# Stage 1 of a four-layer network: one x tile on its own transfer, one bias product, ternary weights two steps earlier, the first turns of stage 2 in four banks

## The reference

```python
# layer 1: attention inside one row (32 heads of 16, 4 groups)
q = x @ Wq + bq; kv = x @ Wkv + bkv          # 512 and 128 columns
scores = einsum(q, k) / 4; out = softmax(scores) * v
# layer 2: feed-forward with ternary weights
quant(w) = clip(round(w / (mean(|w|) + 1e-8)), -1, 1)
h = sigmoid(x @ quant(w1).T) * (x @ quant(w2).T); f = h @ quant(w3).T   # 1408 hidden
# layer 3: causal attention with rotary positions, 16 heads of 32
# layer 4: silu(x @ w_gate) * (x @ w_up), the 2 largest of each 4 kept, @ w_down
```

## Time and profile before

| | |
|---|---|
| median of 3 runs | 1456.96 us (1456.81 to 1458.09) |
| the profiled execution's own time | 1460.82 us |
| its span, first to last instruction | 1458.8 us |
| mean granted TensorE clock | 0.977 of full |
| busy: PE, DVE, ACT, POOL | 1362.8, 1019.7, 662.4, 684.3 us |
| step 0 to the first product of `up2(0)` | 0 to 128.25 us |

### The profile page before, as it was taken

One profiled execution on the slowest core, in us unless ns is written; L12 is line 12 of the kernel. 1 busy time (PEld: TensorE's weight loads), 2 busy tenths in 40 slices (PEclk: granted clock), 3 DMA queues, 4 the chain that ended last, 5 costly groups with the idle time before them and its releaser, 6 DMA issues.

```text
span 1458.8 us, 19653 instructions
## 1 busy us (share of the span) xinstructions
PE 1362.8 (93%) x7214; PEld 926.6 (64%) x7238; DVE 1019.7 (70%) x2118; ACT 662.4 (45%) x1150; POOL 684.3 (47%) x836
## 2 busy tenths in 40 slices
PE   6997999999989899989999998989999999999997
PEld 5984445555455454554554436878888888878885
DVE  5896566665657777777857645487678867887776
ACT  5664233232323544445543574455545545454442
POOL 2575122312313223234232357567768768666862
PEclk9998999999998899999999999999999999999999
DMA  9100210112213111133120401532223222332300
GB/s 341 49 1 1 73 58 1 44 58 89 79 44 95 52 45 37 45 85 106 38 74 1 139 30 59 195 122 87 87 87 144 87 103 102 143 125 106 116 29 29
DMA packets 46248, 116.87 MB, mean 80 GB/s; under 512 B 3399, under 2 KB 4425, under 8 KB 42313
## 3 DMA queue, kind: packets, MB, share of 16 engines
q1 hardware_dynamic: 45080, 114.31, 23.2%
q10 hardware_dynamic: 1072, 1.31, 0.3%
HBM read 92.28 MB, written 23.07 MB: 79 GB/s over the span
## 4 chain that ended last, share of the span: by engine, by line
PE 64%; DVE 24%; ACT 5%; POOL 3%; issue 2%; DMA 1%; SPq 0%; POOLq 0%; DVEq 0%; ACTq 0%
PE PS L1634 63%; DVE cm L615 5%; DVE PS L817 2%; DVE SM L631 2%; DVE SM L627 2%; PE PS L1643 1%; DVE tm L615 1%; DVE SM L621 1%; ACT EX L1218 1%; POOL SM L1449 1%; DVE hm L624 1%; DVE RD L853 1%; DMA rw<-in_L_ffn_w_up 1%; DVE SM L632 1%; DVE qb L621 1%
## 5 line engine op out<-in xcount | busy, mean ns | idle before, releaser
L1218 ACT ACTIVATE EX<-PS 128x512 f32<-128x512 f32 (+3 forms) x384 | 170.2, 495 | 167.9 <-PE PS L1634 166.5
L1449 POOL TENSOR_TENSOR SM<-SM 128x1 f32<-128x1 f32 x256 | 108.6, 427 | 258.0 <-DVE SM L621 248.0
L1449 POOL TENSOR_TENSOR ws_g<-rw,ws_g 128x512 fp32r<-128x512 f32 x64 | 137.2, 2144 | 131.2 <-ACT ws_g L1045 131.2
L1634 PE MATMUL PS<-KG,QG 96*128 96x512 f32 (+3 forms) x384 | 144.8, 399 | 27.1 <-DVE SM L817 15.8
L1553 POOL TENSOR_SCALAR_AFFINE_SELECT EX<-EX 128x128 f32<-128x128 f32 x256 | 75.8, 306 | 198.3 <-ACT EX L1218 194.5
L817 DVE CUSTOM_DVE_ANT_0 PS<-PS,MW 128x128 f32<-128x128 f32 (+3 forms) x256 | 122.2, 498 | 35.0 <-PE PS L1634 34.2
L1634 PE MATMUL PS<-QG,KG 98*128 98x512 f32 (+3 forms) x384 | 136.9, 384 | 4.9 <-ACT EX L1218 2.8
L1418 ACT ACTIVATE ab<-hm 128x512 f32<-128x512 f32 x64 | 40.5, 633 | 209.0 <-DVE hm L615 209.0
L1634 PE MATMUL PS<-ws_d,HH 128*128 128x512 f32 x528 | 125.7, 389 | 0.2 <-DVE HH L615 0.2
L627 DVE TENSOR_REDUCE SM<-PS 128x1 f32<-128x512 f32 x128 | 87.3, 682 | 50.7 <-PE PS L1634 50.4
L1634 PEld LDWEIGHTS PS<-QG,KG 98*128 98x128 f32 x384 | 72.8, 194 | 77.7 <-issue 48.1
(11 more groups left out here) (201 smaller groups left out, 2819.4 us busy)
## 6 DMA issues: line engine op xcount, KB each, us to landing
rw<-in_L_ffn_w_gate SPq DMA_DIRECT2D x16, 1024.0 KB, 5.1
rw<-in_L_ffn_w_up SPq DMA_DIRECT2D x16, 1024.0 KB, 5.1
rw<-in_L_ffn_w_down SPq DMA_DIRECT2D x16, 1024.0 KB, 7.0
QG<-qs SPq DMA_DIRECT2D x48, 256.0 KB, 4.3
raw<-in_L_ffn_w SPq DMA_DIRECT2D x3, 2816.0 KB, 19.8
qs<-stg SPq DMA_DIRECT2D x16, 512.0 KB, 3.8
xA<-xs SPq DMA_DIRECT2D x2, 2048.0 KB, 9.1
ys<-xA SPq DMA_DIRECT2D x4, 1024.0 KB, 5.8
```

Of the source, the lines that this page charges most:

```text
L1218: e.activation(EX[:, n % 16, 0:W], PS[:, score_bank(n), 0:W], ACT.Exp, scale=ISQ, bias=0.0).then_inc(S["ex"], 1)
L1449: return e.tensor_tensor(out, a, b, op)
L1634: return e.matmul(out, l, r, start=start, stop=stop, skip_group_check=free)
```

## The change

1. x tile 1 has its own transfer straight behind tile 0; tiles 2 and 3 follow where 1 to 3 were. In step 1, DVE takes tile 1's statistics before `weights1`, not after.
2. raw1 is issued only when raw0 has landed. Tiles 8 to 15 stay behind it.
3. The bias rows are loaded at partitions 0 and 32 (two transfers more); the high half is in row 0 and the low half in row 32 of a tile that DVE first fills with zeros (33 x 640), and one product per bank over 33 rows takes the place of two. ACT makes two copies in place of one.
4. Sums, means, compares, turns and copies of the ternary weights are all two steps earlier (the first sums one step); statistics and norms of the first four tiles of layer 2 too. The last turns are now all ahead of `up2(0)`.
5. The first two turns of stage 2 use banks 4 and 5 and wait only for tile 14's scores; the next two use 6 and 7.
6. DVE's `softmax1(6)` and ACT's norms of tiles 10 and 11 move from step 20 to behind the first four turns.
7. In every layernorm of the kernel (128 of them), DVE no longer writes the negated mean; POOL's last instruction forms the shift from mean and scale in one `tensor_scalar` in place of a `tensor_tensor`.

```diff
@@ sp_program
             e.dma_start(xA[:, 0:1, :], xin[:, 0:1, :]).then_inc(S["d_x0"], 16)
-            e.dma_start(BR[0:1, :, 0:256], bq_d...).then_inc(S["d_b"], 16)
-            e.dma_start(BR[0:1, :, 256:320], bkv_d...).then_inc(S["d_b"], 16)
+            e.dma_start(xA[:, 1:2, :], xin[:, 1:2, :]).then_inc(S["d_x1"], 16)
+            for r in (0, 32):
+                e.dma_start(BR[r:r + 1, :, 0:256], bq_d...).then_inc(S["d_b"], 16)
+                e.dma_start(BR[r:r + 1, :, 256:320], bkv_d...).then_inc(S["d_b"], 16)
             w.wait_ge(S["d_wqa"], 32)
-            e.dma_start(xA[:, 1:4, :], xin[:, 1:4, :]).then_inc(S["d_x1"], 16)
+            e.dma_start(xA[:, 2:4, :], xin[:, 2:4, :]).then_inc(S["d_x2"], 16)
             e.dma_start(raw[0]..., w1_d...).then_inc(S["d_raw0"], 16)
             e.dma_start(xA[:, 4:8, :], xin[:, 4:8, :])
+            w.wait_ge(S["d_raw0"], 16)
             e.dma_start(raw[1]..., w2_d...).then_inc(S["d_raw1"], 16)
@@ sums: 4, 4, 5, 5 (were 5, 5, 6, 6) for m = 0; else
-    range(4 * m + 3, 4 * m + 7)
+    range(4 * m + 2, 4 * m + 6)
@@ bank3, freed
-            return 6 + misc_no[t] % 2 if t in misc_no else top_no[t] % 3
+            return (misc_no[t] + 4 if misc_no[t] < 2 else 6 + misc_no[t] % 2) if t in misc_no else top_no[t] % 3
+            if x < 2 and t in misc_no:
+                return "pr", NT - (x < 0)
@@ dve_program
-                ts1(col(n, 2), col(n, 1), float(eps), ALU.add)
-                ts1(col(n, 3), col(n, 0), -1.0, ALU.mult).then_inc(S[sem], 1)
+                ts1(col(n, 2), col(n, 1), float(eps), ALU.add).then_inc(S[sem], 1)
+            e.memset(BRH[:, :, :].bitcast(F32), 0.0)
-                        tt(BRH[:, 1], BR[:, :, :], BRH[:, 0], ALU.subtract).then_inc(S["wlo"], 1)
+                        tt(BRH[32:33], BR[32:33], bhi[32:33], ALU.subtract).then_inc(S["wlo"], 1)
             for s in range(21):
-                if 16 <= s < 20: ... stats(32 + s - 16, xt(s - 16), EPS, "mv3")
-                if s == 1: weights1()
-                if s in (7, 11, 15): gamma_sum((s - 7) // 4)
-                if s in (8, 12, 16): gamma((s - 8) // 4)
+                if 14 <= s < 18: ... stats(32 + s - 14, xt(s - 14), EPS, "mv3")
+                if s in (6, 10, 14): gamma_sum((s - 6) // 4)
+                if s in (7, 11, 15): gamma((s - 7) // 4)
                 phase1(s)
-                if 0 <= s - 9 < 12: quantize(s - 9)
+                if s == 1: weights1()
+                if 0 <= s - 7 < 12: quantize(s - 7)
@@ act_program
-                        cp(BRH[:, 0], BR[:, :, :]).then_inc(S["whi"], 1)
+                        cp(BRH[0:1], BR[0:1])
+                        cp(bhi[32:33], BR[32:33]).then_inc(S["whi"], 1)
@@ pool_program
-                tt(col(n, 5), col(n, 3), col(n, 4), ALU.mult).then_inc(S[sem], 1)
+                e.tensor_scalar(col(n, 5), col(n, 0), col(n, 4), -1.0, ALU.mult, ALU.mult).then_inc(S[sem], 1)
@@ pe_program
                 for a in range(2):
-                    for hl in range(2):
-                        mm(out[a], onesr[0:1, :], BRH[0:1, hl, a, :], hl == 0, False)
+                    mm(out[a], onesr[0:33, :], BRH[:, a, :], True, False)
             for s in range(21):
-                if s in (8, 12, 16): gamma((s - 8) // 4)
-                quantized(s - 11, 2)
+                if s < 20: quantized(s - 9, 2)
                 ... project1, transpose4 ...
-                quantized(s - 10, 0)
-                quantized(s - 10, 1)
+                quantized(s - 8, 0)
+                quantized(s - 8, 1)
+                if s in (6, 10, 14): gamma((s - 6) // 4)
@@ ahead of up2(0), and in its first turns
-            for i in range(4): turn_x(i)
+            turn_x(0); turn_x(1); quantized(11, 2); turn_x(2); turn_x(3)
-                if n == 0: quantized(10, 2); quantized(11, 0)
-                if n == 1: quantized(11, 1); quantized(11, 2)
```

More of the change, by code:

```diff
@@ L216, in network @@
         turns = []
[L217 to L220, removed]
+        for s in range(21):
+            turns += [("t", gdone[s - 9] + 2)] if 0 <= s - 9 < 12 and groups[s - 9] == 3 else []
+            turns += [("t", gdone[s - 8] + k) for k in range(2)] if 0 <= s - 8 < 12 else []
+            turns += [("s", (s - 6) // 4)] if s in (6, 10, 14) else []
         turn_no = {t: n for n, t in enumerate(turns)}
@@ L224, in turn_bank @@
             return 2 + turn_no[t] % 2
-        sums = [(s, m, k) for m in range(3) for k, s in enumerate((5, 5, 6, 6) if m == 0 else range(4 * m + 3, 4 * m + 7))]
+        sums = [(s, m, k) for m in range(3) for k, s in enumerate((4, 4, 5, 5) if m == 0 else range(4 * m + 2, 4 * m + 6))]
         jobs = {10 + c: ("q", c) for c in range(4)}
@@ L707, in phase1 @@
                     scores1(at_k[5])
-                if 7 in at_k and at_k[7] % 2:
+                if 7 in at_k and at_k[7] % 2 and step != 20:
                     softmax1(at_k[7] // 2)
@@ L1111, in phase1, with norms1 @@
                     norm(xn1[:, i % 2, :], xt(i), i).then_inc(S["xn1"], 1)
-                if 9 in at_k and at_k[9] % 2:
-                    for i in (at_k[9] - 1, at_k[9]):
-                        w.wait_ge(S["rs2"], i + 1)
-                        w.wait_ge(S["x1"], max(0, i - 1))
-                        norm(yn1[:, i % 2, :], o0[:, i % 4, :], 16 + i).then_inc(S["yn1"], 1)
+                if 9 in at_k and at_k[9] % 2 and step != 20:
+                    norms1(at_k[9])
+            def norms1(last):
+                for i in (last - 1, last):
+                    w.wait_ge(S["rs2"], i + 1)
+                    w.wait_ge(S["x1"], max(0, i - 1))
+                    norm(yn1[:, i % 2, :], o0[:, i % 4, :], 16 + i).then_inc(S["yn1"], 1)
             def norm2(i):
@@ L1356, in split_w @@
                 cp(hi, src).then_inc(S["h" + ("w" if kind == "d" else kind)], 1)
-            for i in range(4):
-                turn_x(i)
+            turn_x(0)
+            turn_x(1)
+            quantized(11, 1)
+            turn_x(2)
+            turn_x(3)
+            norms1(11)
             for n in range(44):
@@ L1933, in down4 @@
                         last.then_inc(S["dd"], 1)
-            for i in range(4):
-                turn_x(i)
+            turn_x(0)
+            turn_x(1)
+            quantized(11, 2)
+            turn_x(2)
+            turn_x(3)
             for n in range(44):
```

76 lines of the change are left out of this document (36 added, 40 removed).

## The result

| | before | after |
|---|---|---|
| median | 1456.88 us (1456.45 to 1458.09, 4 runs) | 1446.72 us (1444.73 to 1449.17, 4 runs) |
| ratio, 95% interval | | 0.9923 [0.9909, 0.9938] |
| profiled execution, its span | 1460.82, 1458.8 us | 1444.73, 1443.0 us |
| `up2(0)` starts | 128.25 us | 120.34 us |
| `up2(2)` starts | 142.45 us | 130.67 us |

The change takes 10.2 us; 10.4 were forecast, and 1446.5 us as the time. The interval of the ratio lies clear of 1, so the change is faster, by 0.8%.

The account below looks back on a forecast made before the run. Stage 1 was taken as PE-bound to 44 us, then DVE-bound to 128; 2.0 + 1.3 - 1.2 + 2.75 + 1.75 + 0.7 = 7.3 us at `up2(0)`, plus 2.8 and 0.3, gave 10.4 us: 1446.5 us, range 1441.5 to 1452.

Parts of the forecast that it names:

- moved turns: On PE, the last four groups move ahead of `up2(0)` into idle holes, bringing `up2(2)` 2.8 us more.
- Rival C: POOL's new two-scalar instruction is slow; 1.2 us more per set on the path spends the advance; chance 0.05.
- The clock: At `up2(0)`, PE's clock taken to be low again, so no term; if not, 2.95 us more.
- rival A: Clock stays at 2.4 GHz through `up2(0)`, 2.95 us more gain, 1443.5 us; chance 0.27.
- Rival B: In stage 1, DVE or ACT waits, such as for a late raw1, eat the advance: about 1451 us; chance 0.18.
- Rival D: PE and DVE are so evenly loaded that the wait only changes its name; nothing moves; chance 0.05.

Follow-up runs that it names:

- run 2: Changed kernel with tiles 1 to 3 again in one transfer behind the weights and tile 1's statistics after `weights1`: 1453.33 us.
- run 3: Changed kernel with four bias products per tile again, the 33-row product made twice so the bias counts double: 1452.12 us.
- run 1: Changed kernel with raw1 issued at once, without waiting for raw0: 1443.58 us.
- run 10: Changed kernel with idle PE products, seven behind the last ternary turn and nine ahead of `up2(0)`, to keep the clock up: 1447.37 us.
- run 12: Changed kernel with raw1 issued at once and idle PE products keeping the clock up: median of 6 1449.54 us, ratio to the kernel before 0.9936.
- run 5: Changed kernel without early tile 1, raw1's wait, the halved bias products and the shorter DVE statistics; earlier compares, banks and order stay: 1451.57 us.
- run 6: Kernel before plus early tile 1, raw1's wait, fewer bias products and shorter DVE statistics, without earlier compares, new banks or order: 1456.72 us.
- run 4: Changed kernel with DVE writing the negated mean again and POOL multiplying two columns: 1447.24 us.
- run 8: Changed kernel with `softmax1(6)` and the norms of tiles 10 and 11 back in step 20: 1448.33 us.
- run 7: Changed kernel with the four turns ahead of `up2(0)` in banks 6 and 7, waiting for tile 15's scores: 1446.84 us.
- run 9: Changed kernel with one extra unused DVE statistics instruction ahead of each of the 12 compare pairs: 1450.91 us.
- run 11: Changed kernel unchanged, again in five rounds: median of 6 1449.34 us, ratio to the kernel before 0.9932; profiled execution 1450.58 us.

## Why the prediction was right

The direction and the places are right: the changed kernel has `up2(0)` at 120.34 (121 forecast), `up2(2)` 10.33 us after it (11.5), step 7 at 32.36 (32), one bias product for each bank, and the gain is found again at the end. That the total is right to 0.2 us is luck, at two places. In the sum for `up2(0)` edits 2 and 3 were put 1.2 and 1.0 us too low, edit 7 and the group of edits 4 and 6 0.7 and 0.8 too high. And `up2(2)` is 1.7 us further ahead than forecast, while the median at the end is not.

The third column is what was read at `up2(0)`. The fourth is an estimate: the same less the difference that already stood at tile 1 without the edit being its cause.

| term | forecast | at `up2(0)` | start taken out | by |
|---|---|---|---|---|
| edit 1, tile 1 early | 2.0 | 2.30 | 1.96 | run 2 |
| edit 3, bias products | 1.3 | 1.93 | 2.3 | run 3 |
| edit 2, raw1 behind raw0 | -1.2 | -0.48 | 0.0 | runs 1, 10 and 12 |
| edits 4, 5 and 6 together | 2.75 + 0.7 | 2.07 alone, 3.70 on top | 2.6 and 2.6 | runs 5, 6 |
| edit 7, DVE instruction | 1.75 | 1.03 | 1.06 | run 4 |
| edit 6, undone singly | (0.7) | 1.59 | 1.48 | run 8 |
| edit 5, undone singly | none | 1.30, given back by the clock | 1.46 | run 7 |
| moved turns, `up2(0)` to `up2(2)` | 2.8 | 3.87, 1.25 of them in `up2(0)` | | profile after |

With the start taken out, edits 1, 2, 3 and 7 and the group of 4, 5 and 6 add up to 7.9 us, and 7.91 were measured.

**What bounds stage 1.** The prediction took the change from PE to DVE from busy shares of windows, at 44 us. By the chain of waits it is at 74 us in the kernel before and at 59 us in the changed one. Edits 3 and 7 are mis-sized by this.

**Edit 1** was sized rightly; `project1(0)` came at 14.30, not 14.1, ACT's bias copies 0.74 apart in place of 0.62.

**Edit 3** counted three tiles, 1.3 us. Seven tiles have their bias products on the chain, 2.3 us: the first three as forecast in kind (0.53, 0.29 and 0.29), and four more that the prediction had put under DVE's queue. That the first three do not show at step 7 is because DVE's split waits for raw1 there. The assumption of the same time for 33 rows and one is shown right.

**Edit 2** costs 0.36 to 1.16 us at step 7 (1.2 forecast) and nothing in the sum. Step 7's split is not on one chain with `up2(0)`: PE's queue is, and does not wait there. The step that failed is adding a delay of DVE at step 7 in full to advances of PE's queue.

**Edit 7** was counted 25 times 0.07. From 59.27 to 120.34, where DVE is the bound, there are 19 sets, and the instructions take 0.21 us with the negation and 0.15 without it: 19 times 0.06 is 1.1, measured 1.06. That POOL's instruction takes 0.06 more is small beside it. Rival C, which wanted 1.2 us or more for each set, is refuted.

**Edit 4**: DVE's idle time from step 7 to `up2(0)` falls by 3.4 us (2.75 forecast), its work by 2.8 (1.75 + 0.7 forecast), by the windows. At `up2(0)` edits 4, 5 and 6 bring 2.6 us together, 3.45 forecast. How these divide is not shown: edits 5 and 6 undone singly already come to 2.9, and edit 4 was never run without them. What edit 4 does show by itself is behind `up2(0)`: the moved turns bring 3.87 - 1.25 = 2.6 us there, 2.8 forecast.

**Edits 5 and 6.** Edit 5 had no term; it moves `up2(0)` and nothing from `up2(3)` on. Edit 6's norms on ACT were not hidden, as the prediction had it: ACT's copy stands ahead of DVE's split.

**The clock** was taken to be as before, with rival A (it stays up) 2.95 us better. It came between: it was high when `up2(0)` began and 0.50 from 121.2 to 124.3, and `up2(0)` took 5.15 us in place of 6.40. These 1.25 us are what `up2(2)` has over the forecast: 11.78 us ahead for 10.1 forecast, of which 0.6 come from `up2(0)`. That the end has 10.2 and not 12 comes from behind that place. In the two profiled executions the first exponential of stage 3 is 12.62 us ahead, the last 13.17, and the first compare of stage 4 over 128x1536 11.77 (934.30 and 922.53). Then stage 4 of the kernel before lost 4.7 us more up to its last group of compares (1394.60 for 1378.14). One long compare (7.75 us) is 3 of them; 1.45 more are between 960.85 and 992.19, where run 5 has them too, for a reason that was not looked into. So the end differs by 16.1 in these two executions. The lowest times differ by 11.7 (1456.45 and 1444.73) and, in the later rounds, by 12.2 (1456.44 and 1444.28), which is what `up2(2)` has. The medians, 10.2 and 9.6, are less because the changed kernel's times reach further above its lowest; that long compares do this in the executions without a trace is likely and not shown.

**Rival B** (waits eat the advance) had its condition half met: raw1 landed 0.6 us later than forecast and ACT waited 1.23 for it, but it cost nothing at `up2(0)`. **Rival D** is refuted by 7.9 us of advance.

## What to carry to other kernels

Where a pipeline changes its bound on the way, an early loss or gain is not worth its size at the place where it is seen: up to 1.16 us at step 7's split were nothing at the end of the stage, and an edit that showed nothing there was worth 1.9. Take the place where the bound changes from the chain of waits, not from busy shares. Multiply a cost for each step by the number of steps in which its engine is the bound; one run with a known piece of extra work on that engine tells it (4.47 of 7.3 us here).

Before two kernels are compared at a late place, compare them at the first common one. The start of this kernel varies by some tenths (tile 1 at 20.44 to 21.04), and read without it, one edit seemed to cost 0.48 us and the parts seemed to help one another.

To move work two steps ahead pays by the idle time of the engine in the steps that take it in, and in the chain it shows mostly at the end, in the steps that have lost the work.

## What the runs showed of the hardware

A compare on DVE, `cm<-ab` over 128x1536, which takes up to 2.9 us as a rule, took 7.6 to 8.3 us now and then, whatever the kernel: once or more in before and in runs 2, 3, 4, 6, 7, 9, 10, 11 and 12, and never in after and in runs 1, 5 and 8, out of 15 such instructions each. DVE and POOL get in each other's way there, and either can be the one that is slowed: where such a compare takes 2.54 us (changed kernel, 1111.71), POOL's products over 128x512 in and behind it take 2.82, 2.53 and 2.00 us, and where it takes 8.09 (run 11, 1111.43), they take 1.34 to 1.61 and the compare ends 1.6 us behind the last of them. The same is seen at the long compares of before and of runs 3, 7 and 10, with POOL's products at 1.27 to 1.64. What decides which of the two is slowed was not tried. One long compare in the middle of stage 4 costs 3.0 to 3.1 us at the end (runs 3, 7, 10 and 11), one near its start cost 1.2 (run 9, at 954). Two executions of one kernel that agree within 0.02 us at 130 us then differ by 6 at 1445.

The clock at the start of stage 2 falls or stays in kernels that differ little, and the idle time directly ahead of `up2(0)` does not decide it alone. With 2.27 us idle ahead (changed kernel, runs 1, 2, 3, 4, 5 and 9) the granted clock was 0.54 to 0.71 over `up2(0)`, with 3.69 us (run 8) it was 0.72, with 1.42 us it was 0.53 in the kernel before, 0.72 in run 6 and 1.00 in run 7, and with 0.32 us (run 10) 1.00. At full speed `up2(0)` takes 3.46 us, at 0.53 it took 6.40. To start it 1.3 us earlier behind a longer pause was worth nothing (run 7).
